# One fused transformer block with mixture of experts: token weights folded in pieces, beta in four column groups, and a reordered opening

## The chip, the cores and the metric

The kernel runs on one core of one Trainium2 chip. The metric is the device time of one execution in microseconds. The kernel before takes 736.07 us (median of 3 runs, 735.96 to 736.86). The engines are TensorE (PE, with its weight loads PEld), VectorE (DVE), ScalarE (ACT), GpSimd (POOL) and SyncE (SP), which issues all loads and stores.

## What is computed

The input is 32 images of 128x128x3. The reference does three steps, all in float32:

```
tokens = patchify(concat(x, x shifted by one pixel in 4 directions), 16)    # 64 tokens x 3840 features per image
h = layernorm(tokens, eps 1e-3) * gamma + beta;  h = h @ W + b              # 192 wide
h = h + attention(layernorm(h))     # 12 heads of 16, each 64x64, three softmax kernels (here equal),
                                    # inverse of the middle one by 6 Newton steps
h = h + experts(layernorm(h))       # 16 experts of width 128 (8) and 256 (8), top 8, gelu
```

## The kernel before

Tokens go in 16 tiles of 128 (two images each). The five shifts are not made in memory: the weights W of the five taps are scaled by gamma and summed into one small weight `weff` of 8 chunks of 128 rows, of which 6 are inner pixels and 2 are borders (the "halo"). One more column of `weff` gives the mean. `wsh[:, hh, f, ch]` is half `hh` of the pixels, tap `f`, colour `ch`; chunk `3 * hh + ch` is folded from the five taps f, by VectorE, with the semaphore `folded` counting the 32 operations. The term beta @ W is a chain of 32 matmuls with one column of weights each into row 0 of PSUM bank A; VectorE copies the row to `crow`, TensorE spreads it over 128 partitions, and VectorE adds the bias to give `cvec`. `wsum`, the column sums of `weff`, comes from 8 matmuls with a matrix of ones. An fp32 matmul is two records in the trace.

Each engine has its own program, written out by hand, and they meet by semaphores. After this prologue each runs `iteration(t)`, in which six Newton steps k of tile t are interleaved with work of its neighbours: in the windows of the steps stand the token matmul of tile t + 3 (`tok`, L263), its sums and squares, the hidden value and its normalisation for tile t + 2 (`hidden`, `normed`, then `transpose_xl`, `qk`, `value`, `masked_keys`), the scores, softmax and start matrix of tile t + 1 (`scores`, `less_max`, `transpose_kernel`, `column_sums`, `gram`, `start_newton`), and output and router of tile t - 1. The iterations begin at t = -3, with no Newton work before t = 0. Banks A to D are shared: the scores write all four, so `tok` of a later tile waits for `less_max` (semaphore `sdiff`). The rsqrt steps run on GpSimd, six small operations each.

SyncE issues all loads in one order: gamma and beta (`gbs`, 32 KB), the two halves of the taps (1440 KB each), the halo weights (192 KB), the bias spread over the partitions (96 KB), constants (169 KB), transposed x and x of tile 0 (512 KB each), the table of copies (512 KB), seven attention weights (880 KB together), the pair for tile 1, the expert weights (5376 KB), and then the pairs of tiles 2 to 15, each behind a wait for the token matmul and the squares of the tile two before. After the last tile come the experts, 24 chunks for each of four groups of tiles.

Of the kernel before, what the change touches and what calls it, by code (L numbers as in the profile page):

```python
# [11 lines left out]
CH = 8  # L12
# [28 lines left out]
def vit_block_kernel(nc, x, xt, ws, wh, gb, tok_b, wqk, wv, wp, bp, rw, w1, w2, const, copies, out):  # L41
    with ExitStack() as ctx:
# [18 lines left out]
        crow = sb("crow", [1, DIM])  # L61
# [64 lines left out]
        const_loaded, wsh_top_loaded, wsh_loaded, mult_loaded = sems("const_loaded wsh_top_loaded wsh_loaded mult_loaded")  # L126
# [25 lines left out]
        @block.sync  # L152
        def _(sp):
            def tile_loads(t):
                b = t % 2
                if t >= 2:
                    sp.wait_ge(tok_done, t - 1)
                sp.dma_start(xtb[:, b], xt[t]).then_inc(xt_loaded[b], 16)
                if t >= 2:
                    sp.wait_ge(sq_ready, t - 1)  # L160
                sp.dma_start(xin[b], x[t]).then_inc(x_loaded[b], 16)

            sp.dma_start(gbs[:], gb).then_inc(wsh_top_loaded, 16)
            sp.dma_start(wsh[:, 0], ws[:, 0]).then_inc(wsh_top_loaded, 16)
            sp.dma_start(wsh[:, 1], ws[:, 1]).then_inc(wsh_loaded, 16)
            sp.dma_start(whalo[:], wh).then_inc(wsh_loaded, 16)
            sp.dma_start(tokb[:], tok_b.partition_broadcast(P)).then_inc(wsh_loaded, 16)
            sp.dma_start(cst[:], const).then_inc(const_loaded, 16)
            tile_loads(0)
            sp.dma_start(mult[:], copies).then_inc(mult_loaded, 16)  # L170
            sp.dma_start(wqk_a[:], wqk[0:DA, :]).then_inc(attw_loaded, 16)
            sp.dma_start(wqk_b[:], wqk[DA:DA + P, :]).then_inc(attw_loaded, 16)
            sp.dma_start(wv_a[:], wv[0:DA, :]).then_inc(attw_loaded, 16)
            sp.dma_start(wv_b[:], wv[DA:DA + P, :]).then_inc(attw_loaded, 16)
            sp.dma_start(wp_sb[:], wp).then_inc(attw_loaded, 16)
            sp.dma_start(bp_sb[:], bp.partition_broadcast(P)).then_inc(attw_loaded, 16)
            sp.dma_start(rw_sb[:], rw).then_inc(attw_loaded, 16)
            tile_loads(1)
            sp.dma_start(w1_a[:], w1[0:DA, :]).then_inc(ffw_loaded, 16)
            sp.dma_start(w1_b[0:DB, :], w1[DA:DIM, :]).then_inc(ffw_loaded, 16)  # L180
            sp.dma_start(w1_b[DB:P, :], w1[DA:DIM, :]).then_inc(ffw_loaded, 16)
            sp.dma_start(w2_sb[:], w2.rearrange("(c p) n -> p c n", p=P)).then_inc(ffw_loaded, 16)
            for t in range(2, NT):
                tile_loads(t)
            with sp.Fori(0, NT // GT) as g:
                sp.wait_ge(expert_added, (g + 1) * EXPERTS + 2)
                sp.dma_start(out[bass.ds(g * GT, GT)].rearrange("t p n -> p t n"),
                             acc[:, bass.ds(g * GT, GT), :]).then_inc(out_stored, 16)
            sp.wait_ge(out_stored, 16 * (NT // GT))
# [64 lines left out]
        def _(pe):  # L254
# [142 lines left out]
            def first_window(k, t):  # L397
                if k == 0 and on(t + 1):
                    scores(t + 1)
                if k == 1 and on(t - 1):  # L400
                    out_heads(t - 1)
                if k == 1 and on(t + 3):
                    tok(t + 3, 0, 2)
                if k == 2 and on(t + 1):
                    transpose_kernel(t + 1)
                if k == 2 and on(t + 3):
                    tok(t + 3, 2, 4)
                if k == 3 and on(t + 1):
                    transpose_sums(t + 1)
                    gram(t + 1)  # L410
                if k == 4 and on(t + 1):
                    spread_denominators(t + 1)
                if k == 5 and on(t + 2):
                    qk(t + 2)

            def second_window(k, t):
                if k == 1 and on(t - 1):
                    project(t - 1)
                if k == 2 and on(t + 3):
                    tok(t + 3, 4, CH)  # L420
# [6 lines left out]
                if k == 5 and on(t + 2):  # L427
                    value(t + 2)

            def iteration(t):  # L430
                for k in range(STEPS):
                    if on(t):
                        newton(k, 0, t, 0)
                        newton(k, 0, t, 1)
                    first_window(k, t)
# [5 lines left out]
            n = 0  # L441
            for hh in range(2):
                if hh == 0:
                    pe.wait_ge(wsh_top_loaded, 32)
                else:
                    pe.wait_ge(wsh_loaded, 48)
                for f in range(15):
                    pe.matmul(A[0:1, 0:DIM], gbs[:, 1, hh * 15 + f:hh * 15 + f + 1], wsh[:, hh, f // 3, f % 3, :],  # L448
                              start=(n == 0), stop=False)
                    n += 1  # L450
            pe.matmul(A[0:1, 0:DIM], gbs[:, 1, 30:31], whalo[:, 0, :], start=False, stop=False)
            pe.matmul(A[0:1, 0:DIM], gbs[:, 1, 31:32], whalo[:, 1, :], start=False, stop=True).then_inc(beta_done, 1)
            pe.wait_ge(crow_ready, 1)
            pe.wait_ge(ones_set, 1)
            pe.matmul(B[:, 0:DIM], ones[0:1, :], crow[:], start=True, stop=True).then_inc(cbc_done, 1)
            pe.wait_ge(folded, 32)
            pe.wait_ge(mean_set, 1)
            for c in range(CH):
                last = pe.matmul(D[:, 0:DIM], ones[:], weff[:, c, 0:DIM], start=(c == 0), stop=(c == CH - 1))
            last.then_inc(wsum_done, 1)  # L460
# [4 lines left out]
            for t in range(-3, NT + 1):  # L465
# [42 lines left out]
        def _(act):  # L508
# [72 lines left out]
            def first_window(k, t):  # L581
# [6 lines left out]
                if k == 5 and on(t + 2):  # L588
                    copy_q(t + 2)

            def second_window(k, t):
# [10 lines left out]
                if k == 5 and on(t + 2):  # L602
                    copy_value(t + 2)

            def iteration(t):
                for k in range(STEPS):
                    if on(t):
                        newton(k, 0, t, 0)
                        newton(k, 0, t, 1)
                    first_window(k, t)  # L610
# [5 lines left out]
            act.wait_ge(zeros_set, 2)  # L616
            for t in range(-3, NT):
# [21 lines left out]
        def _(dve):  # L639
# [141 lines left out]
            def window(k, t):  # L781
# [4 lines left out]
                if k == 1 and on(t - 1):  # L786
                    residual_norm(t - 1)
                if k == 2 and on(t + 1):
                    dve.wait_ge(kt_done, 2 * t + 4)
                    column_sums(t + 1, B, 4, 2, colsum_b)  # L790
                if k == 2 and on(t + 2):
# [18 lines left out]
                if k == 5 and on(t + 2):  # L810
# [4 lines left out]
            def iteration(t):  # L815
                for k in range(STEPS):
                    if on(t):
                        newton_sum(k, t, 0)
                        newton_sum(k, t, 1)
                    if on(t) and k == STEPS - 1:  # L820
# [6 lines left out]

            n = 0
            for hh in range(2):
                if hh == 0:  # L830
                    dve.wait_ge(wsh_top_loaded, 32)
                else:
                    dve.wait_ge(wsh_loaded, 48)
                for f in range(5):
                    for ch in range(3):
# [9 lines left out]
                        n += 1  # L845
            for c in range(2):
# [131 lines left out]
```

## Time and profile before

| | |
|---|---|
| median of 3 runs | 736.07 us |
| the profiled execution's own time | 739.34 us |
| its span, first to last instruction | 737.6 us |
| TensorE matmul busy | 680.3 us |
| VectorE busy | 496.5 us |
| ScalarE busy | 356.3 us |
| GpSimd busy | 108.2 us |
| mean granted TensorE clock | 0.981 |

Times of the rows are microseconds from the start of the span, and those marked mean are nanoseconds. An engine's share is an average over the span; which engine sets the time in a stretch is read from the chain of waits, which follows the last instruction back to what released it at each step.

### The profile page before, as it was taken

To read this page: it belongs to the slowest core of one execution; us is meant where nothing else is said; L and a number is where in the kernel's file an instruction comes from. 1 tells how busy PE (TensorE), PEld (TensorE's weight loads), DVE (VectorE), ACT (ScalarE), POOL (GpSimd) and SP (SyncE) were. 2 spreads that over 40 slices of the span, in tenths; PEclk is the share of its full clock that TensorE was granted. 3 is DMA by queue.
4 is the path that set the end of the run, shared out by engine and by line. 5 is a ranking of instruction groups with operands and counts; after the bars stand their busy time and mean duration, and the time that the engine had idled before them with its cause. 6 is when DMAs were issued, how large, how long until landed. Compare 5 with 4: busy or idle time off the path is not lost.

```text
span 737.6 us, 30455 instructions
## 1 busy us (share of the span) xinstructions
PE 680.3 (92%) x13218; PEld 595.5 (81%) x13218; DVE 496.5 (67%) x1354; ACT 356.3 (48%) x921; POOL 108.2 (15%) x328
## 2 busy tenths in 40 slices
PE   5668999999999999999999999869999999999996
PEld 2457888788888888888888878748898898998986
DVE  5257778777878878877778877447456546646644
ACT  0125664655655655555555655534334344434432
POOL 0122123123123123223123211110000000000000
PEclk9969999999999999999999999979999999999999
DMA  8951111011011011111000000000000000000000
GB/s 311 300 182 60 61 48 44 33 44 48 33 60 33 32 60 32 32 61 32 32 4 5 4 4 4 4 1 2 1 1 21 0 0 21 0 0 21 0 0 22
DMA packets 12244, 30.48 MB, mean 41 GB/s; under 512 B 1120, under 2 KB 7392, under 8 KB 11616
## 3 DMA queue, kind: packets, MB, share of 16 engines
q1 hardware_dynamic: 12128, 28.73, 11.9%
q8 instruction: 97, 1.59, 0.9%
q14 instruction: 19, 0.16, 0.1%
HBM read 27.16 MB, written 1.57 MB: 39 GB/s over the span
## 4 chain that ended last, share of the span: by engine, by line
PE 76%; DVE 14%; ACT 5%; issue 3%; DMA 1%; POOL 1%; DVEq 0%; ACTq 0%; SPq 0%; POOLq 0%
PE ps L364 24%; PE ps L493 17%; PE ps L484 15%; PE ps L263 6%; DVE uu L734 3%; DVE sq L653 2%; PE ps L277 2%; PE ps L382 2%; PE ps L314 2%; DVE rf L741 2%; ACT qq L557 2%; PE ps L448 2%; PE ps L278 1%; ACT rr L561 1%; PE ps L375 1%
## 5 line engine op out<-in xcount | busy, mean ns | idle before, releaser
L884 DVE SCALAR_TENSOR_TENSOR acc<-ps,comb,acc 128x192 f32 x256 | 89.2, 411 | 90.3 <-PE ps L493 90.3
L493 PE MATMUL ps<-w_sb,work 128*128 128x192 f32 x768 | 139.9, 326 | 0.5 <-ACT work L633 0.3
L364 PE MATMUL ps<-rr 64*64 64x64 f32 x3840 | 131.4, 221 | 6.0 <-issue 3.3
L493 PEld LDWEIGHTS ps<-w_sb,work 128*128 128x128 f32 x768 | 129.2, 189 | 9.5 <-issue 1.7
L364 PEld LDWEIGHTS ps<-rr 64*64 64x64 f32 x3840 | 119.8, 136 | 18.7 <-ACT rr L561 10.6
L557 ACT ACTIVATE qq<-ps 128x384 f32<-128x384 f32 x192 | 92.3, 490 | 66.7 <-PE ps L364 64.7
L734 DVE SCALAR_TENSOR_TENSOR uu<-rr,qq 128x384 f32<-128x384 f32 x160 | 87.9, 559 | 50.8 <-ACT qq L557 44.6
L633 ACT ACTIVATE work<-ps 128x512 f32<-128x512 f32 x96 | 57.3, 597 | 133.6 <-PE ps L484 133.6
L561 ACT ACTIVATE rr<-ps 128x384 f32<-128x384 f32 x160 | 73.9, 490 | 80.6 <-PE ps L364 79.8
L364 PE MATMUL ps<-uu,qq 64*64 64x64 f32 x4608 | 96.6, 224 | 16.1 <-DVE uu L734 13.9
L364 PEld LDWEIGHTS ps<-uu,qq 64*64 64x64 f32 x4608 | 80.6, 134 | 33.9 <-DVE uu L734 30.6
L263 PE MATMUL ps<-weff,xtb 128*128 128x193 f32 x256 | 53.9, 347 | 3.9 <-DVE se L690 2.4
L484 PE MATMUL ps<-xhi,wah 128*128 x96 | 47.5, 495 | 1.1 <-ACT rt L579 1.1
L263 PEld LDWEIGHTS ps<-weff,xtb 128*128 128x128 f32 x256 | 42.7, 197 | 6.8 <-issue 4.7
L484 PE MATMUL ps<-xhi,wal 128*128 x96 | 38.2, 398 | 0.0
L484 PE MATMUL ps<-xhi,wb 128*128 x96 | 38.1, 397 | 0.0
L484 PE MATMUL ps<-xlo,wah 128*128 x96 | 38.1, 397 | 0.0
L484 PE MATMUL ps<-xlo,wb 128*128 x96 | 37.9, 394 | 0.0
L863 DVE TENSOR_TENSOR wal<-w_a,wah 128x128 fp32r<-128x128 f32 x98 | 28.1, 286 | 8.6 <-ACT wb L622 6.5
L863 DVE TENSOR_TENSOR wb<-w_b,wb 64x128 fp32r<-64x128 f32 x98 | 28.4, 290 | 3.1
L206 POOL TENSOR_SCALAR st<-st 128x1 f32<-128x1 f32 x16 | 6.4, 402 | 162.5 <-DVE st L653 162.5
L622 ACT ACTIVATE wah<-w_a 128x128 fp32r<-128x128 f32 x98 | 29.6, 302 | 0.0
(136 smaller groups left out, 1026.8 us busy)
## 6 DMA issues: line engine op xcount, KB each, us to landing
xtb<-xt_dram SPq DMA_DIRECT2D x16, 512.0 KB, 3.5
work<-x_dram SPq DMA_DIRECT2D x16, 512.0 KB, 3.4
wsh<-ws_dram SPq DMA_DIRECT2D x2, 1440.0 KB, 7.8
w_sb<-w_dram SPq DMA_DIRECT2D x1, 2304.0 KB, 26.3
w_a<-w_dram SPq DMA_DIRECT2D x1, 1536.0 KB, 13.2
w_b<-w_dram SPq DMA_DIRECT2D x2, 768.0 KB, 17.7
out_dram<-acc SPq DMA_DIRECT2D x4, 384.0 KB, 2.7
mult<-copies_dram SPq DMA_DIRECT2D x1, 512.0 KB, 12.8
```

Of the source, the lines that this page charges most:

```text
L263: last = pe.matmul(C[:, 0:DIM + 1], xtb[:, t % 2, c, :], weff[:, c, :], start=(c == 0), stop=(c == CH - 1))
L277: pe.matmul(D[:, w * P:w * P + P], wqk_a[:, w * P:w * P + P], xlt[:, 0, :], start=True, stop=False)
L364: last = pe.matmul(ps[z:z + 64, 2 * lane + i, 64 * j:64 * j + 64], lhs[r, lane, i, j, :], rhs[r, lane, i, j, :], start=True, stop=True)
L484: last = pe.matmul(ps[:, c % 2, :], w[:, k, :], xs[:, half, tok], start=(n == 0), stop=(n == 4))
L493: last = pe.matmul(ps[:, 2 + 2 * (e % 2) + j // 2, (j % 2) * DIM:(j % 2 + 1) * DIM], hid[:, c % 4, j * P:(j + 1) * P], w2_sb[:, c, :], sta ...
L557: act.activation(qq[:, lane].rearrange("p i h n -> p i (h n)"), ps[:, 2 * lane:2 * lane + 2, 0:LC], ACT.Copy).then_inc(q_ready, 1)
L561: act.activation(rr[:, lane].rearrange("p i h n -> p i (h n)"), ps[:, 2 * lane:2 * lane + 2, 0:LC], ACT.Copy, scale=0.25).then_inc(r_ready, 1)
L622: act.activation(w[:, c % 3, :], raw[:, c % HID * P:(c % HID + 1) * P], ACT.Copy).then_inc(whi_ready, 1)
L633: act.activation(hid[:, c % 4, :], ps[:, c % 2, :], ACT.Gelu_apprx_tanh).then_inc(gelu_done, 1)
L734: dve.scalar_tensor_tensor(out=uu[:, lane], in0=src[:, lane], scalar=3.0, in1=qq[:, lane], op0=ALU.mult, op1=ALU.add).then_inc(u_ready, 1)
L863: dve.tensor_tensor(w[a:P, k, :], raw[a:P, col:col + P], high[a:P, k, :].bitcast(F32), ALU.subtract).then_inc(wlo_ready, 1)
L884: last = dve.scalar_tensor_tensor(out=a, in0=ps[:, 2 + 2 * (e % 2) + j // 2, (j % 2) * DIM:(j % 2 + 1) * DIM].unsqueeze(1), scalar=comb[:, ...
```

## The change

The taps are loaded in ten pieces of 288 KB, each with its own semaphore, and the fold and the beta matmuls wait for each piece. Beta's 32 matmuls use a weight block of 32 equal columns at one of four column positions in turn, so each column group sums eight terms over 32 partitions; `crow` becomes the whole bank, and the spread is a matmul of ones with all 128 rows, divided by 32 where the bias is added. TensorE's token matmul of tile 0 and the weight sums run in three pieces (chunks 0 to 2, 3 to 5, 6 and 7) between the halves of beta and after them, and iteration -3 falls away on TensorE and VectorE, with `token_sums(0)` and `variance(0)` written into VectorE's prologue. ScalarE does one dummy square ahead of its first iteration. Iterations before t = 0 run `tok` in one piece in window k = 1 and `hidden` ahead of the column sums. The projections, copies and masked keys of tile 1 leave iteration -1 and stand in iteration 0 behind the first squares of tile 0. The order of loads changes: constants and transposed x of tile 0 between the tap pieces, the bias later, and the pairs of tiles 2 and 3 ahead of the expert weights.

```diff
-            sp.dma_start(gbs[:], gb).then_inc(wsh_top_loaded, 16)
-            sp.dma_start(wsh[:, 0], ws[:, 0]).then_inc(wsh_top_loaded, 16)
-            sp.dma_start(wsh[:, 1], ws[:, 1]).then_inc(wsh_loaded, 16)
-            sp.dma_start(whalo[:], wh).then_inc(wsh_loaded, 16)
-            sp.dma_start(tokb[:], tok_b.partition_broadcast(P)).then_inc(wsh_loaded, 16)
+            def taps(half, f0, f1):
+                for f in range(f0, f1):
+                    sp.dma_start(wsh[:, half, f], ws[:, half, f]).then_inc(tap_loaded[half][f], 16)
+
+            sp.dma_start(gbs[:], gb).then_inc(gamma_loaded, 16)
+            taps(0, 0, 5)
+            taps(1, 0, 2)
             sp.dma_start(cst[:], const).then_inc(const_loaded, 16)
-            tile_loads(0)
+            sp.dma_start(xtb[:, 0], xt[0]).then_inc(xt_loaded[0], 16)
+            taps(1, 2, 5)
+            sp.dma_start(whalo[:], wh).then_inc(halo_loaded, 16)
+            sp.dma_start(xin[0], x[0]).then_inc(x_loaded[0], 16)
             sp.dma_start(mult[:], copies).then_inc(mult_loaded, 16)
+            sp.dma_start(tokb[:], tok_b.partition_broadcast(P)).then_inc(tokb_loaded, 16)
...
-            tile_loads(1)
+            for t in range(1, 4):
+                tile_loads(t)
...
-            for t in range(2, NT):
+            for t in range(4, NT):
                 tile_loads(t)
...
                 if k == 1 and on(t + 3):
-                    tok(t + 3, 0, 2)
+                    tok(t + 3, 0, 2 if t >= 0 else CH)
...
-                if k == 2 and on(t + 3):
+                if k == 2 and on(t + 3) and t >= 0:
                     tok(t + 3, 2, 4)
...
-                if k == 5 and on(t + 2):
+                if k == 5 and on(t + 2) and t != -1:
                     qk(t + 2)
...
                         newton(k, 0, t, 1)
+                    if t == 0 and k == 0:
+                        qk(1)
+                        value(1)
                     first_window(k, t)
...
+            def beta(n, w):
+                z = 32 * (n % 4)
+                return pe.matmul(A[z:z + 32, 0:DIM], gbs[:, 1, n:n + 1].to_broadcast([P, 32]), w, start=(n < 4), stop=(n >= 28),
+                                 tile_position=(0, z))
+
+            def beta_taps(half):
+                for f in range(5):
+                    pe.wait_ge(tap_loaded[half][f], 16)
+                    for ch in range(3):
+                        beta(half * 15 + 3 * f + ch, wsh[:, half, f, ch, :])
+
+            def first_tok(c0, c1):
+                pe.wait_ge(folded, (15, 30, 32)[c0 // 3])
+                for c in range(c0, c1):
+                    last = pe.matmul(C[:, 0:DIM + 1], xtb[:, 0, c, :], weff[:, c, :], start=(c == 0), stop=(c == CH - 1))
+                if c1 == CH:
+                    last.then_inc(tok_done, 1)
+                for c in range(c0, c1):
+                    last = pe.matmul(D[:, 0:DIM], ones[:], weff[:, c, 0:DIM], start=(c == 0), stop=(c == CH - 1))
+                if c1 == CH:
+                    last.then_inc(wsum_done, 1)
+
+            pe.wait_ge(gamma_loaded, 16)
+            beta_taps(0)
+            pe.wait_ge(ones_set, 1)
+            pe.wait_ge(mean_set, 1)
+            pe.wait_ge(xt_loaded[0], 16)
+            first_tok(0, 3)
+            beta_taps(1)
+            pe.wait_ge(halo_loaded, 16)
+            beta(30, whalo[:, 0, :])
+            beta(31, whalo[:, 1, :]).then_inc(beta_done, 1)
+            first_tok(3, 6)
+            first_tok(6, CH)
             pe.wait_ge(crow_ready, 1)
+            pe.matmul(B[:, 0:DIM], ones[:], crow[:], start=True, stop=True).then_inc(cbc_done, 1)
...
-            for t in range(-3, NT + 1):
+            for t in range(-2, NT + 1):
                 iteration(t)
...
+                    if t == 0 and k == 0:
+                        copy_q(1)
+                        copy_value(1)
...
             act.wait_ge(zeros_set, 2)
+            act.activation(st[:, 23:24], ot[:, 0, 0:1], ACT.Square)
...
+                if k == 2 and on(t + 2) and t < 0:
+                    hidden(t + 2)
...
+                    if t == 0 and k == 0:
+                        masked_keys(1)
...
             dve.wait_ge(beta_done, 1)
-            dve.tensor_copy(crow[:], A[0:1, 0:DIM]).then_inc(crow_ready, 1)
-            dve.wait_ge(cbc_done, 1)
-            dve.tensor_tensor(cvec[:], B[:, 0:DIM], tokb[:], ALU.add).then_inc(cvec_ready, 1)
+            dve.tensor_copy(crow[:], A[:, 0:DIM]).then_inc(crow_ready, 1)
             dve.wait_ge(wsum_done, 1)
             dve.tensor_copy(wsum[:], D[:, 0:DIM]).then_inc(wsum_ready, 1)
+            token_sums(0)
+            dve.wait_ge(cbc_done, 1)
+            dve.wait_ge(tokb_loaded, 16)
+            dve.scalar_tensor_tensor(out=cvec[:], in0=B[:, 0:DIM], scalar=1.0 / 32, in1=tokb[:],
+                                     op0=ALU.mult, op1=ALU.add).then_inc(cvec_ready, 1)
+            variance(0)
             dve.wait_ge(cvec_ready, 1)
-            for t in range(-3, NT):
+            for t in range(-2, NT):
                 iteration(t)
```

## Rows read from the trace of the kernel before

**Rows 1.** Chain of waits, 0 to 90 us: start, duration, what, records.

```profile
1.18 6.31 DMA wsh<-ws_dram
7.53 12.66 PE ps L448 x60
...
21.87 2.82 PE ps L459 x16
24.71 0.37 DVE wsum L854
...
28.53 1.28 ACT L512
...
31.12 1.23 DVE sq L653
...
38.48 0.47 PE ps L271
...
44.55 0.70 PE ps L306 x24
...
50.23 1.54 PE ps L314 x6
51.77 3.20 PE ps L263 x12
```

**Rows 2.** Busy times by stretch; after the engines come granted clock, DMA share, GB/s.

```profile
9.00:12.00 3.00, 3.00 (x11) 1.16 (x10) 3.00 (x11) 0.00 (x0) 0.00 (x0) 1.00 0.92 242
...
15.00:18.00 3.00, 3.00 (x20) 1.59 (x19) 3.00 (x10) 0.00 (x0) 0.00 (x0) 1.00 1.02 395
...
33.00:36.00 3.00, 0.00 (x0) 0.00 (x0) 1.38 (x5) 0.00 (x0) 1.36 (x7) 1.00 1.06 263
36.00:39.00 3.00, 0.52 (x2) 0.29 (x2) 0.78 (x2) 0.00 (x0) 1.90 (x6) 0.68 1.10 330
...
54.00:57.00 3.00, 2.46 (x63) 1.93 (x61) 1.65 (x8) 0.00 (x0) 1.52 (x6) 0.98 0.33 96
```

**Rows 3.** Timeline of SyncE's queue: start and duration of each issue.

```profile
1.65 0.42 SPq L165 DMA_DIRECT2D wsh<-ws_dram  x1
...
3.65 0.62 SPq L158 DMA_DIRECT2D xtb<-xt_dram  x1
...
9.77 0.90 SPq L177 DMA_DIRECT2D rw_sb<-rw_dram  x1
```

**Rows 4.** Loads: size and microseconds to landing, from stretches with one issue each.

```profile
gbs<-gb_dram SPq DMA_DIRECT2D x1, 32.0 KB, 1.8
...
wsh<-ws_dram SPq DMA_DIRECT2D x1, 1440.0 KB, 9.2
...
xtb<-xt_dram SPq DMA_DIRECT2D x1, 512.0 KB, 11.6
...
rw_sb<-rw_dram SPq DMA_DIRECT2D x1, 16.0 KB, 10.4
...
xtb<-xt_dram SPq DMA_DIRECT2D x1, 512.0 KB, 16.1
```

**Rows 5.** Timeline of VectorE, the fold of one half's later taps.

```profile
8.29 4.04 DVE L843 SCALAR_TENSOR_TENSOR weff<-wsh,gbs,weff 128x192 f32<-128x192 f32 x12
```

**Rows 6.** Timeline of TensorE, head outputs of tile 0 in four column groups.

```profile
90.96 0.64 PE L375 MATMUL ps<-rf,y_t 128*32 128x64 f32 x24
91.53 0.43 PE L263 MATMUL ps<-weff,xtb 128*128 128x193 f32 x1
```

**Rows 7.** Timeline, 56 to 72 us: start matrices, first squares, tile 1's maxima.

```profile
57.99 1.03 DVE L726 TENSOR_TENSOR r<-cst,m 128x384 f32<-128x384 f32 x2
...
60.28 1.61 PE L364 MATMUL ps<-r 64*64 64x64 f32 x48
...
63.14 0.69 DVE L688 TENSOR_REDUCE sst<-ps 128x8 f32<-128x512 f32 x1
```

More of the change, by code:

```diff
@@ L60, in vit_block_kernel @@
         weff = sb("weff", [P, CH, DIM + 1])
-        crow = sb("crow", [1, DIM])
+        crow = sb("crow", [P, DIM])
         ones = sb("ones", [P, P])
@@ L124, in sems @@
             return [sem(n) for n in names.split()]
-        const_loaded, wsh_top_loaded, wsh_loaded, mult_loaded = sems("const_loaded wsh_top_loaded wsh_loaded mult_loaded")
+        const_loaded, gamma_loaded, halo_loaded, tokb_loaded, mult_loaded = sems(
+            "const_loaded gamma_loaded halo_loaded tokb_loaded mult_loaded")
+        tap_loaded = [[sem(f"tap_loaded_{half}_{f}") for f in range(5)] for half in range(2)]
         x_loaded, xt_loaded = sems("x_even_loaded x_odd_loaded"), sems("xt_even_loaded xt_odd_loaded")
@@ L418, in second_window @@
                     project(t - 1)
-                if k == 2 and on(t + 3):
+                if k == 2 and on(t + 3) and t >= 0:
                     tok(t + 3, 4, CH)
@@ L426, in second_window @@
                     logits(t - 1)
-                if k == 5 and on(t + 2):
+                if k == 5 and on(t + 2) and t != -1:
                     value(t + 2)
@@ L439, in iteration @@
                     second_window(k, t)
[L441 to L451, printed above, removed]
@@ L452, in _ @@
-            pe.matmul(A[0:1, 0:DIM], gbs[:, 1, 31:32], whalo[:, 1, :], start=False, stop=True).then_inc(beta_done, 1)
-            pe.wait_ge(crow_ready, 1)
[L454 to L459, printed above, removed]
@@ L460, in _ @@
-            last.then_inc(wsum_done, 1)
+            def beta(n, w):
[7 more added lines that the diff above has]
+                        beta(half * 15 + 3 * f + ch, wsh[:, half, f, ch, :])
@@ L587, in first_window @@
                     save_y(t + 1)
-                if k == 5 and on(t + 2):
+                if k == 5 and on(t + 2) and t != -1:
                     copy_q(t + 2)
@@ L601, in second_window @@
                     squares(t + 3)
-                if k == 5 and on(t + 2):
+                if k == 5 and on(t + 2) and t != -1:
                     copy_value(t + 2)
@@ L790, in window @@
                     column_sums(t + 1, B, 4, 2, colsum_b)
-                if k == 2 and on(t + 2):
+                if k == 2 and on(t + 2) and t >= 0:
                     hidden(t + 2)
@@ L809, in window @@
                     router_max(t - 1)
-                if k == 5 and on(t + 2):
+                if k == 5 and on(t + 2) and t != -1:
                     masked_keys(t + 2)
@@ L826, in _ @@
             dve.wait_ge(scrap_set, 1)
+            dve.wait_ge(gamma_loaded, 16)
             n = 0
             for hh in range(2):
[L830 to L833, printed above, removed]
                 for f in range(5):
+                    dve.wait_ge(tap_loaded[hh][f], 16)
                     for ch in range(3):
@@ L845, in _ @@
                         n += 1
+            dve.wait_ge(halo_loaded, 16)
             for c in range(2):
```

## The prediction

> **What bounds the kernel now.** I read the page's busy shares first: TensorE is busy 680 of 738 us, as the table shows. Then the chain of waits in order of time, which shows that this share is an average over two regimes. From about 60 us on, the chain is nearly all TensorE with short VectorE links, and the change touches nothing in it but the first of sixteen tile iterations. Before that the chain is a prologue in which one engine at a time works: the first half of the token weights lands at 7.5, 60 beta matmul records run to 20.2, the weight sums run 21.9 to 24.7, tile 0's token matmul fills the time to the table load at 28.53, which takes 1.28, and so on down to tile 0's scores at 44.55 and its transposes at 50.23 [rows 1]. Third, TensorE's clock by the stretches: the records ran at 11 per 3 us at 9 to 12 us and at 20 per 3 us at 15 to 18 us, so the start is at the lower of the two levels (1.2 and 2.4 GHz) although the page grants it 1.00; the granted clock later falls within 36 to 39 (0.68) after 33 to 36 without a matmul and is 0.98 in 54 to 57 [rows 2]. Fourth, the issues and landings of the loads [rows 3, 4]. So what is taken from the prologue shifts all the rest, because TensorE has no slack later; what merely fills a gap there brings nothing.
>
> **The change part by part.** Times are of the one profiled execution (span 737.6, its own time 739.34); the median of the plain runs is 736.07, 3.27 lower. I take the difference over to the median unchanged.
>
> *Taps instead of halves.* The halves landed at 1.18 + 6.31 = 7.5 and 1.65 + 9.2 = 10.85 [rows 1, 3, 4]: 1440 KB in 3.4 us, so 288 KB in 0.67 us. Ten issues instead of two cost SyncE 0.42 each and some 0.05 between them [rows 3], less than 0.67, so the queue stays ahead. Counting back from 7.5, the first tap lands at 4.8. VectorE folds a first tap in 0.78 and a later one in 4.04 / 4 = 1.01 [rows 5], slower than they land: 4.8 + 2 x (0.78 + 4.04) + 0.55 for the halo = 15.0, where it ended at 18.7. This takes 3.7 us from the fold, but TensorE decides, next.
>
> *Beta in four column groups, tile 0's matmul and the sums between.* Tile 0's transposed x now lies behind 2217 KB instead of 3369: 7.5 + (2729 - 1472) x 0.00234 = 10.4, where it landed at 3.65 + 11.6 = 15.25 [rows 3, 4]. The first half of beta hides under the taps. At 10.4 TensorE starts chunks 0 to 2 of token matmul and sums: 12 records of 0.18 at the higher clock (2.82 / 16 for 192 columns, [rows 1]), 0.36 at the lower. I let the clock rise at 13.2 as it did before: 7.6 records by then, 4.4 after, end 13.9. Second half and halo of beta: 34 records. No row shows column groups at 192 columns; the head outputs, 128x32 weights and 64 columns, start 24 records in (0.64 - 0.22) / 23 = 0.018 each [rows 6]; three times that for three times the columns is 0.054, so 1.8 us and 15.8. Without any overlap it is 0.16 each, 5.4 us; with no cost at all it is 0. I take 1.8, the nearest row. Chunks 3 to 7: 20 records x 0.18 = 3.6, so the weight sums are ready at 19.4 instead of 24.7: -5.2 (rounded by the issue gaps). If the clock rises only near 16.6, it is 21; if the groups do not overlap, 23; if all is at the higher clock and beta is free, 16.5. The broadcast matmul grows from one row to 128 and stays 0.6 with its copy, beside the squares.
>
> On the switch between column groups and the whole array, the same rows show a group of 128x32 matmuls between 64x64 and 128x128 ones with the next token record at 91.53, 0.57 after the first of the 24, so no gap beyond a record. The Trainium skill ("TensorEngine Tiling (Array Packing)", Key Properties) says that changing the tiling mode drains TensorE. By it the three switches added here would cost three drains, by the row at most 3 x 0.22 = 0.7 us; I count none.
>
> *Token matmul off the path.* It stood from 24.71 + 0.37 to 28.3, just before the table load, behind the sums [rows 1]: -3.2. *Dummy square on ScalarE*: the 1.28 us table load goes to the start, under the loads: -1.3. With these the squares of tile 0 start at 20.1 and the variance at 21.4 instead of 31.12: -9.7. x and the copies table (landed by about 15.4) are not late. Tile 1's token matmul comes at about 21.6, when its x lands (same bytes ahead as before), ends at 24.5 and hides under tile 0's rsqrt on GpSimd.
>
> *Variance to scores*: 31.12 to 44.55 is 13.4 us, the same instructions in the same order. Of it some 5.5 us from 38.48 on are matmuls at the lower clock. They would take half as long at the higher one, -2.7; TensorE stands idle from 24.5 to 28.8 before them, as it stood (longer, 6.6 us) before, so I let the clock fall as it did. A little more of them falls behind the rise: -0.3. Scores to the normed kernel (50.18): no change.
>
> *Token matmul of tile 2 in one piece, ahead of tile 0's transposes.* It starts at about 37.3 (before, 47.6). With part at the lower clock it takes 4.4 us (2.9 to 5.8 are the ends), so the transposes start at 41.8, 1.7 after their input, where they waited for nothing. But then they run at the higher clock (0.8, not 1.54 us) and the 3.20 us of tokens behind them, which held up the sums' transpose until 54.8, are gone; what is late next is the copy and column sum, 1.2 us. From kernel ready to the first r0 tile it was 8.3 (50.2 [rows 1] to 58.5, half of the two r0 writes [rows 7]) and becomes 7.2: -1.1, between -2.5 and +0.3. The earlier hidden(1) lies beside the copies.
>
> *Tile 1's projections behind the first squares.* Before, the squares started at 60.28, 1.8 after their first input [rows 7]. Now they start at once, but 1.6 us of squares, 1.5 of q and k, 0.9 of values, the copy and the scores follow in order before tile 1's maxima: 5.2 instead of 4.6 after r0 (63.14 before): +0.6; bounds 0 and +1.0. ScalarE has the 1.1 us squares of tile 2 and the y copies queued ahead of the first quotient copy, and VectorE waits for that one.
>
> *Loads of tiles 2 and 3 ahead of the expert weights.* Tile 2's transposed x, issued once tile 0's token matmul was done (28.2), took 16.1 us behind 5.4 MB of weights and landed at 44.3 [rows 4]; now it is wanted at 37.3, so without this the gain would end there (+7). With it, it lands by 24. Tile 3's x waits on SyncE for tile 1's squares (about 31), and the expert weights behind it then land at about 53, wanted after 500. Tile 4's x lies behind them, wanted after 80. Cost 0.
>
> Sum: -9.7 - 0.3 - 1.1 + 0.6 = -10.5; of the profiled execution 739.34 - 10.5 = 728.8, of the median **725.6**.
>
> **The rivals.**
> A. *The clock stays up.* The new prologue packs TensorE's work closer, so the fall need not come before tile 0's projections (-2.7) and tile 2's tokens (-1.4). Against it stands the 4.3 us hole; for it, that 6.6 us stood there before. Gives 725.6 - 3.5, about 722.
> B. *TensorE's opening is late*: clock up at 16.6 or groups that hardly overlap, sums at 22 to 23. +3, partly given back as the clock is then up in the token matmul: about 728.5.
> C. *Small loads do not overlap: slower.* If a tap paid the whole of a small load's time (gamma and beta's 32 KB took 1.8 us from issue to landing, [rows 4]) and the next began behind it, a tap would take 1.8 + 0.67 = 2.5 us. The ten taps end near 26, and tile 0's x and the copies table, five loads further, near 38 instead of 15.4. The variance starts then, 7 us later than before, and the seven attention loads add 14 more: some 750. It decides from 2.1 us per tap, where the copies table lands at 29.8, when the squares started. Against: nine loads of 16 to 512 KB, 1904 KB in all (tile 0's x, the copies table, the seven attention loads), landed in the 4.9 us between 15.25 and 9.77 + 10.4 = 20.2 [rows 3, 4], as fast per KB as the halves. The Trainium skill ("DMA: Bandwidth & Descriptors", Bandwidth) advises batching loads to 1 MiB or more for 75% of peak, and puts 64 KB at 32% of it. By it 288 KB taps would arrive at something like half rate, and an estimate from its figures delays the queue by some 7 us, nearer B than C.
> D. *The gain isn't there*: a later wait of the prologue takes it all, such as the attention weights (20.2) or a load. All that I found are earlier than their users; 736.
>
> **How the numbers follow.** Forecast (-8.5 to -12.5) 0.70; A 0.10; B 0.12; C 0.03; D 0.03; the rest, small gains, 0.02. Less than 0.2% (1.5 us) is what a measurement can't tell from no change. Faster 0.94, same 0.03, slower 0.03. The range for 8 in 10 takes the forecast's own bounds and most of A and B: 722.3 to 729.2.
>
> **What would show it.** Fold's first record near 4.8 and its end near 15; first token record near 10.4; wsum copy at 19.5; variance at 21.4; tile 0's scores near 34.5; less_max of tile 1 near 52.5; then all as before with -10.5. Wrong if beta's records start 0.16 apart or more, if the taps land over 0.9 us apart, if tile 2's tokens wait for a load, or if the iterations from tile 1 on take longer than they did.

## The result and the profile after

| | before | changed |
|---|---|---|
| median of 6 plain runs | 736.27 us (735.48 to 738.45) | 730.61 us (728.24 to 732.48) |
| ratio, 95% interval | | 0.9918 [0.9893, 0.9944] |
| profiled execution: span | 737.6 | 726.4 |
| mean granted clock | 0.981 | 0.984 |

The change makes the kernel 5.7 us faster. I forecast 10.5 (725.6 us), with a range of 722.3 to 729.2: the sign is right, the size is not, and the range misses.

The page after, busy times:

```profile
PE 673.6 (93%) x13218; PEld 593.3 (82%) x13218; DVE 496.8 (68%) x1354; ACT 356.3 (49%) x922; POOL 109.5 (15%) x328
```

The chain of waits of the changed kernel in its first 80 us (start, duration, what, records), which answers [rows 1]:

```profile
4.97 6.65 DMA xtb<-xt_dram
...
11.87 2.27 PE ps L467 x6
14.13 1.92 PE ps L471 x6
16.06 1.92 PE ps L455 x34
17.98 1.18 PE ps L467 x6
...
20.79 0.67 PE ps L471 x4
21.48 0.36 DVE wsum L887
...
23.23 1.23 DVE sq L685
...
36.75 1.16 PE ps L315 x24
...
40.29 4.53 PE ps L272 x16
44.82 0.67 PE ps L323 x6
...
49.58 0.57 DVE r L758
50.20 2.58 PE ps L373 x48
```

The steps are there in the order in which I had put them. But the first six token records take 2.27 us and the next six on the same tile 1.18: the same work at the lower and at the higher of TensorE's two levels, 1.2 and 2.4 GHz. The scores take 1.16 where they took 0.70, and the first squares 2.58 where they took 1.61 [rows 7].

Busy times by stretch of the changed kernel, which answer [rows 2]; the third figure from the end is the granted clock:

```profile
12.00:15.00 3.00, 3.00 (x10) 3.00 (x11) 2.60 (x8) 0.00 (x0) 0.00 (x0) 1.00 1.05 411
...
27.00:30.00 3.00, 0.00 (x0) 0.00 (x0) 1.26 (x6) 0.00 (x0) 1.62 (x7) 1.00 0.58 176
30.00:33.00 3.00, 1.87 (x7) 1.47 (x8) 0.60 (x1) 1.42 (x2) 0.49 (x1) 0.51 0.00 1
...
39.00:42.00 3.00, 1.71 (x5) 1.74 (x6) 2.41 (x6) 1.05 (x2) 0.28 (x2) 0.50 1.13 287
...
48.00:51.00 3.00, 1.48 (x30) 1.18 (x31) 2.66 (x7) 1.89 (x5) 0.00 (x0) 0.92 1.09 327
51.00:54.00 3.00, 3.00 (x40) 2.88 (x37) 1.89 (x4) 1.27 (x4) 1.86 (x4) 0.51 1.11 340
```

At 12 to 15 us the page again grants 1.00 while 10 records fill 3 us, so the start is at the lower level, as before. Then the clock falls at 30, is 0.50 at 39 to 42, and falls once more near 50.5, behind TensorE's wait for r0. This last fall has no counterpart before, where tile 1's projections filled 57.9 to 60.3.

**Two traces differ by 11.2 us and the plain runs by 5.7.** The start of each tile's last Newton sum, which writes the tile `rf`, is read from VectorE's timeline. Those of tile 0 and of tile 15 split the spans:

| | to tile 0's rf | tiles 0 to 15 | rest |
|---|---|---|---|
| before | 84.56 | 396.02 | 257.0 |
| changed | 78.55 | 391.90 | 255.9 |
| difference | -6.0 | -4.1 | -1.1 |

The change touches nothing behind the first column. An even iteration is 26.56 us from rf to rf in both traces; the trace of before has five of 26.9 to 28.9. TensorE's timeline of before shows what is in them: waits for nothing that the profile names, marked issue.

```profile
131.42 1.15 PE L364 MATMUL ps<-rr 64*64 64x64 f32 x33 [0.89 <-issue]
...
159.75 0.62 PE L364 MATMUL ps<-rr 64*64 64x64 f32 x13 [0.97 <-issue]
...
```

The profiled execution of before was a long sample (739.34 against a median of 736.27) and that of the change the shortest of its six (728.24 against 730.61), so the 11.2 that seem to confirm the -10.5 of my sum do so by chance. The first column agrees with the plain runs: -6.0 here, and -4.9 with the second trace of the changed kernel (79.67, k_after below).

### The profile page after: what moved, and what is told of

It reads as the page before. It is cut to its first block, busy times and chain, and to the rows that moved or that the text cites. A ratio compares the mean times of both kernels' runs of the same rounds, so it can differ in the third digit from the quotient of the medians.

```text
span 726.4 us, 30474 instructions
## 1 busy us (share of the span) xinstructions
PE 673.6 (93%) x13218; PEld 593.3 (82%) x13218; DVE 496.8 (68%) x1354; ACT 356.3 (49%) x922; POOL 109.5 (15%) x328
## 4 chain that ended last, share of the span: by engine, by line
PE 77%; DVE 13%; ACT 4%; issue 2%; DMA 1%; POOL 1%; SPq 1%; DVEq 0%; ACTq 0%; POOLq 0%
PE ps L373 25%; PE ps L521 17%; PE ps L512 15%; PE ps L272 6%; DVE uu L766 3%; DVE sq L685 2%; PE ps L286 2%; PE ps L391 2%; PE ps L323 2%; ACT qq L585 2%; DVE rf L773 2%; PE ps L287 2%; PE ps L341 1%; ACT rr L589 1%; PE ps L384 1%
## 5 line engine op out<-in xcount | busy, mean ns | idle before, releaser
L766 DVE SCALAR_TENSOR_TENSOR uu<-rr,qq 128x384 f32<-128x384 f32 x160 | 87.8, 559 | 46.9 <-ACT qq L585 41.0
L373 PEld LDWEIGHTS ps<-uu,qq 64*64 64x64 f32 x4608 | 80.3, 134 | 32.8 <-DVE uu L766 29.5
L272 PE MATMUL ps<-weff,xtb 128*128 128x193 f32 x240 | 50.6, 347 | 3.9 <-DVE se L722 2.4
L512 PE MATMUL ps<-xhi,wah 128*128 x96 | 47.6, 495 | 1.1 <-ACT rt L607 1.1
L272 PEld LDWEIGHTS ps<-weff,xtb 128*128 128x128 f32 x240 | 39.9, 196 | 6.6 <-issue 4.5
L654 ACT ACTIVATE wb<-w_b 128x128 fp32r<-128x128 f32 x98 | 29.4, 300 | 0.0
```

Of the source, the lines that this page charges most:

```text
L272: last = pe.matmul(C[:, 0:DIM + 1], xtb[:, t % 2, c, :], weff[:, c, :], start=(c == 0), stop=(c == CH - 1))
L373: last = pe.matmul(ps[z:z + 64, 2 * lane + i, 64 * j:64 * j + 64], lhs[r, lane, i, j, :], rhs[r, lane, i, j, :], start=True, stop=True)
L512: last = pe.matmul(ps[:, c % 2, :], w[:, k, :], xs[:, half, tok], start=(n == 0), stop=(n == 4))
L654: act.activation(w[:, c % 3, :], raw[:, c % HID * P:(c % HID + 1) * P], ACT.Copy).then_inc(whi_ready, 1)
L766: dve.scalar_tensor_tensor(out=uu[:, lane], in0=src[:, lane], scalar=3.0, in1=qq[:, lane], op0=ALU.mult, op1=ALU.add).then_inc(u_ready, 1)
```

## The experiments

Milestones of the profiled executions, in us from the start (VectorE's copy of the weight sums; variance of tile 0; scores of tile 0; its kernel transposes; first squares; first maxima of tile 1):

| | sums | variance | scores | transp. | squares | max 1 | plain median | ratio [95%] |
|---|---|---|---|---|---|---|---|---|
| before | 24.7 | 31.1 | 44.6 | 50.2 | 60.3 | 63.1 | 736.27 | 1 |
| my forecast | 19.5 | 21.4 | 34.5 | 41.8 | 47.3 | 52.5 | 725.6 | |
| changed | 21.5 | 23.2 | 36.8 | 44.7 | 50.2 | 57.1 | 730.61 | 0.9918 [0.9893, 0.9944] |
| k_after | 22.3 | 24.1 | 37.5 | 45.8 | 51.3 | 58.3 | 730.66 | 0.9918 [0.9899, 0.9937] |
| e_back | 21.0 | 22.7 | 36.2 | 43.5 | 50.7 | 53.6 | 728.48 | 0.9906 [0.9871, 0.9940] |
| e_fill | 20.2 | 21.9 | 35.3 | 41.5 | 47.1 | 52.4 | 723.74 | 0.9829 [0.9809, 0.9849] |
| e_back_fill | 20.8 | 22.6 | 33.9 | 40.2 | 47.6 | 50.5 | 725.95 | 0.9859 [0.9839, 0.9878] |
| e_move_only | 23.4 | 29.9 | 42.7 | 48.9 | 57.0 | 62.4 | 737.29 | 1.0003 [0.9987, 1.0018] |
| e_halves | 21.3 | 23.0 | 36.2 | 44.8 | 50.6 | 56.0 | 730.13 | 0.9927 [0.9898, 0.9956] |
| e_onerow | 23.5 | 25.3 | 38.8 | 46.3 | 51.8 | 58.7 | 732.36 | 0.9919 [0.9891, 0.9946] |
| e_loads_late | 21.3 | 23.0 | 36.5 | 50.6 | 56.1 | 63.0 | 736.90 | 1.0009 [0.9990, 1.0028] |
| e_split | 21.9 | 23.6 | 37.1 | 43.2 | 52.1 | 57.5 | 729.97 | 0.9909 [0.9878, 0.9940] |
| e_fill_end | 22.1 | 23.9 | 36.6 | 45.3 | 50.8 | 56.3 | 726.72 | 0.9876 [0.9852, 0.9900] |
| e_best_a | 19.7 | 21.4 | 32.8 | 39.1 | 44.6 | 49.9 | 723.63 | 0.9848 [0.9816, 0.9880] |
| e_best_b | 20.1 | 21.9 | 33.2 | 39.5 | 46.9 | 49.8 | 724.50 | 0.9855 [0.9825, 0.9886] |

The runs of one kernel spread by 2 to 4 us, so ratios that differ by less than 0.3% tell nothing; the milestones do not carry that part of the spread that arises in the iterations. They have a spread of their own: k_after, the same kernel as the changed one, is 0.8 us later at the sums and 1.1 at the maxima, and e_move_only, whose code up to the sums is that of before, copies them at 23.4 and not at 24.7, as its 60 beta records take 11.54 us and not 12.66. So a step from one milestone to the next says more than where a milestone stands.

**k_after**: no edit.

> The changed kernel as it is, as the control for the others of this group and a second trace of it. Theory 1 (the clock: my prologue steps were right in order but TensorE's clock stays low or falls where I had it high) expects 5 to 7 us less than the kernel before, and the same low stretches as in the first trace: 30 to 43 us and about 50.5 to 54 us. Theory 2 (the profile of before was itself some 4 us slow in the iterations, from idle time at TensorE marked issue, and this one less) expects iterations of tiles 3 to 11 that again differ from the even 26.56 us by random amounts that don't recur in the same tiles.

730.66 us, as the first time. The clock's low stretches recur: 0.50 at 36 to 45, and 0.67 at 51 to 54. The beta groups took 2.61 us here and not 1.92, with the same twelve slow token records ahead of them (2.27 and 1.92 us), so the end of the low stretch moves between executions. That the long iterations would not recur in the same tiles was wrong: in all runs without dummy matmuls, but for the first trace of the changed kernel (27.0 and 27.2), the second one from rf to rf takes 27.6 to 27.7 and the ninth 27.4 to 27.7. What is random is the size of the others, up to 30.9 in e_fill_end, whose profiled execution took 732.65 against a median of 726.72.

**e_back**

> Changed kernel, but the projections, copies and masked keys of tile 1 back in the iteration before tile 0's Newton steps, as in the kernel before. Clock theory: these 2.4 us of matmuls fill the hole at 47.3 to 50.2 us, the clock stays up in the first squares (1.6 instead of 2.6 us) and tile 1's maxima start about 1 to 2 us sooner than 57.1: 1 to 2 us faster than the changed kernel. Rival (the move itself is a gain, since the squares start as soon as their input is there): 0.5 to 1.5 us slower than the changed kernel.

```diff
-                if k == 5 and on(t + 2) and t != -1:
+                if k == 5 and on(t + 2):
                     qk(t + 2)          # likewise value, copy_q, copy_value, masked_keys
...
-                    if t == 0 and k == 0:
-                        qk(1)
-                        value(1)       # likewise the copies and masked_keys(1)
```

2.2 us below k_after in the median, but the intervals of the ratios overlap. The trace is clearer: from the first r0 tile to tile 1's maxima it takes 53.58 - 48.44 = 5.1 us, where the changed kernel takes 57.13 - 49.58 = 7.5. TensorE's timeline of e_back:

```profile
48.38 0.49 PE L286 MATMUL ps<-xlt,wqk_a 128*128 128x128 f32 x2 [0.47 <-ACT xlt L541]
...
50.72 1.61 PE L373 MATMUL ps<-r 64*64 64x64 f32 x48
```

The squares start later (50.7, 2.3 after r0) and yet tile 1 is ready sooner: they take 1.61 us and not 2.58.

**e_fill**: 33 dummy matmuls (66 records), whose result nobody reads.

> Changed kernel with dummy matmuls (128x128 ones on 192 columns, into a free PSUM bank, read by nobody) in TensorE's waits of the prologue: one behind each tap's beta matmuls of the first half and four after them, twelve ahead of tile 0's transposes of the normed value, seven behind tile 0's scores, two behind its kernel transposes, three ahead of the first squares. Clock theory: first token pieces at 2.4 GHz (-1.5 to -2), projections of tile 0 at 2.4 GHz (-2.5), scores (-0.5), token matmul of tile 2 (-1.5, partly hidden), first squares and q, k (-1.5 to -2): 5 to 8 us faster than the changed kernel. Rival (the clock does not matter, or dummy matmuls come in the way of real ones): between 0 and 3 us slower.

```diff
+            def fill(n):
+                for _ in range(n):
+                    pe.matmul(ps[:, 0, 0:DIM], ones[:], wsh[:, 0, 0, 0, :], start=True, stop=True)
...
+                    if half == 0:
+                        fill(1)        # behind each tap in beta_taps
...
+            fill(4)                    # behind beta_taps(0)
...
+                if k == 4 and t == -2:
+                    fill(12)           # ahead of transpose_xl(0)
...
+                    if t == -1:
+                        fill(7)        # behind scores(0); fill(2) behind transpose_kernel(0), fill(3) behind transpose_xl(1)
```

6.9 us below k_after in the same group, and the intervals are apart: 0.9829 [0.9809, 0.9849] against 0.9918 [0.9899, 0.9937]. Work was added to TensorE, and what it brought shows in the matmuls behind it, which run in as little as half the time. TensorE's timeline of e_fill:

```profile
12.79 1.15 PE L481 MATMUL ps<-weff,xtb 128*128 128x193 f32 x6
13.77 1.14 PE L485 MATMUL ps<-weff,ones 128*128 128x192 f32 x6
...
23.22 4.42 PE L272 MATMUL ps<-weff,xtb 128*128 128x193 f32 x16 [2.78 <-DMA xtb<-xt_dram]
27.48 4.06 PE L463 MATMUL ps<-wsh,ones 128*128 128x192 f32 x24
...
47.05 1.61 PE L373 MATMUL ps<-r 64*64 64x64 f32 x48 [0.17 <-DVE r L773]
```

The first token pieces and the squares run at the higher level, and so do tile 0's projections (0.22 us for two records, 0.43 in the changed kernel). Tile 1's token matmul does so only in part: it waited 2.78 us for its x, the clock fell at about 23, and the twelve dummies behind it then held up tile 0's transposes by 2 us. Even so tile 1's maxima start at 52.4, where my forecast had them (52.5).

**e_back_fill**: both edits.

> The two edits together. Clock theory: with the clock held up by the dummies the place of tile 1's projections matters little; by my own count from the trace of before (+0.6 for the move) it is 0 to 1 us faster than with the dummies alone. If the move is a gain by itself, 0.5 to 1.5 us slower than with the dummies alone.

By the trace 1.9 us earlier than e_fill at tile 1's maxima, most of it from the clock at tile 1's tokens (2.86 us, not 4.42); by the plain runs 2.2 us later, 0.9859 against 0.9829, intervals that overlap. Neither 0 to 1 faster nor clearly slower: undecided here, and e_best_a and e_best_b take it up.

**e_move_only**: the kernel before with the move of tile 1's projections (the edit of e_back the other way).

> The kernel before with one part of the change alone: tile 1's projections, copies and masked keys behind tile 0's first squares. Clock theory: TensorE then stands from 57.5 to about 59, the clock falls in or behind the first squares, and tile 1's maxima start 1 to 2.5 us later than 63.1; 1 to 2.5 us slower than before. My forecast's own term for it was +0.6; if the move were a gain it would be up to 1 us faster.

1.0003 [0.9987, 1.0018]: no change. I expected 1 to 2.5 us slower. From r0 to tile 1's maxima it takes 62.35 - 56.42 = 5.9 us, where before it took 5.15, so the move costs 0.8 here, close to my term of +0.6 and within its bounds of 0 and 1.0. TensorE stands idle for 1.15 us ahead of the squares, and they take 1.61 us all the same: the clock did not fall, against what I expected.

**e_halves**

> Changed kernel with each half of the taps in one load again, the second right behind the first, and fold and beta waiting for the half. If the pieces bring their time by the early start: the fold starts at 7.5 instead of 4.5 and ends near 18 instead of 15.9, transposed x of tile 0 lands near 12.5 and the weight sums are 1 to 3 us later: 1 to 3 us slower than the changed kernel. If small loads cost rate (part of why transposed x landed at 11.6 and not at 10.4): 0 to 1 us slower only.

```diff
-                for f in range(f0, f1):
-                    sp.dma_start(wsh[:, half, f], ws[:, half, f]).then_inc(tap_loaded[half][f], 16)
+                sp.dma_start(wsh[:, half], ws[:, half]).then_inc(tap_loaded[half][0], 16)
...
-            taps(1, 0, 2)
...
-            taps(1, 2, 5)
+            taps(1, 0, 5)
```

The second half is not right behind the first, as I had written, but behind the constants and tile 0's transposed x. 0.9927 against 0.9918: the pieces bring nothing that can be measured, and the weight sums come at the same time, 21.3. TensorE's timeline of e_halves:

```profile
7.82 2.78 PE L453 MATMUL ps<-wsh,gbs 128*32 128x192 f32 x30 [7.82 <-DMA wsh<-ws_dram]
12.70 1.22 PE L465 MATMUL ps<-weff,xtb 128*128 128x193 f32 x6 [2.10 <-DVE weff L875]
13.76 1.14 PE L469 MATMUL ps<-weff,ones 128*128 128x192 f32 x6
...
17.71 1.25 PE L465 MATMUL ps<-weff,xtb 128*128 128x193 f32 x6 [1.07 <-DVE weff L875]
```

Beta's first half stands in one block of 2.8 us, and the token pieces behind it already run at the higher level, 2.1 us instead of 4.2. They start 0.8 us later, and the last fold (2 us later than in the changed kernel) holds up the next ones by 1.07. What the pieces give the fold they take from the clock.

This run also says something on the later fall. Its order is that of the changed kernel and it has no dummies, and TensorE's idle times ahead of the first squares are the same to the hundredth (1.20, 0.37 and 1.15 us). Yet the clock stays up. Busy times by stretch of e_halves:

```profile
48.00:51.00 3.00, 1.48 (x42) 1.09 (x36) 2.65 (x8) 1.51 (x3) 0.00 (x0) 1.00 1.10 327
51.00:54.00 3.00, 3.00 (x62) 2.81 (x60) 2.24 (x5) 1.74 (x7) 1.58 (x3) 1.00 1.10 337
```

The squares take 1.61 us, and tile 1's maxima come 5.4 us after their start, where the changed kernel took 6.9 and my forecast had 5.2.

**e_onerow**

> Changed kernel with beta summed in one row again (one column of weights, one row of 32 terms), all else as in the change. Its 34 records behind the first token pieces then cost 0.16 to 0.32 each instead of the 1.92 us together that the first trace shows: 5.4 us at the higher clock, so weight sums and tile 0's squares 3.5 to 4.5 us later: 3 to 5 us slower than the changed kernel. Rival (beta off the path): 0 to 1 us slower.

```diff
-                return pe.matmul(A[z:z + 32, 0:DIM], gbs[:, 1, n:n + 1].to_broadcast([P, 32]), w, start=(n < 4), stop=(n >= 28),
-                                 tile_position=(0, z))
+                return pe.matmul(A[0:1, 0:DIM], gbs[:, 1, n:n + 1], w, start=(n == 0), stop=(n == 31))
...
+            pe.matmul(B[:, 0:DIM], ones[0:1, :], crow[:], start=True, stop=True).then_inc(cbc_done, 1)
```

Median 1.7 above k_after, the ratio the same (0.9919): less than the 3 to 5 expected. The 34 records take 5.6 us instead of 1.92, 3.7 more, but the weight sums are only 1.2 to 2.1 later, as the first token pieces, behind a beta of its first half that now takes longer (30 records from 4.58 to 11.23), take 2.1 us instead of 4.2.

**e_loads_late**

> Changed kernel with the pairs of tiles 2 and 3 behind the expert weights again. My forecast said that transposed x of tile 2 lands at 44 and is wanted at about 40: the token matmul of tile 2 waits for it, 4 us later than its 40.3, and stands ahead of tile 0's transposes: 3 to 5 us slower than the changed kernel. Rival (the load is not what was late): 0 to 0.5 us slower.

```diff
-            for t in range(1, 4):
-                tile_loads(t)
+            tile_loads(1)
...
-            for t in range(4, NT):
+            for t in range(2, NT):
                 tile_loads(t)
```

6.2 us above k_after, 1.0009 [0.9990, 1.0028] of before: the whole gain is gone. The chain of waits of e_loads_late:

```profile
20.62 24.76 DMA xtb<-xt_dram
...
45.42 5.34 PE ps L271 x16
50.76 0.67 PE ps L322 x6
```

The load lands at 45.4. I had expected 3 to 5 us here; the +7 of the prediction was the nearer.

**e_split**

> Changed kernel with the token matmul of tiles 0 to 2 in the old pieces (2, 2 and 4 chunks) around the transposes, and the hidden value in its old place. My forecast priced the one piece at -1.1 us: 1 us slower than the changed kernel. Clock theory adds that one piece is a long busy stretch which lifts the clock for the transposes and the column sums: in pieces they run at the lower level, 1 to 2.5 us slower. Rival (tile 0's transposes should not wait behind 4.5 us of tokens): 0.5 to 1.5 us faster.

```diff
-                    tok(t + 3, 0, 2 if t >= 0 else CH)
+                    tok(t + 3, 0, 2)
...
-                if k == 2 and on(t + 3) and t >= 0:
+                if k == 2 and on(t + 3):          # twice; hidden back in its old place
```

0.9909, no difference. The transposes start at 43.2 instead of 44.7, right behind their input, and the sums' transpose at 48.3, 11.2 after the scores, where the changed kernel has 46.7, 9.9 after them; at r0 the difference is 1.6. By tile 1's maxima all of it is made up (20.4 us after the scores in both), since with the late tokens the granted clock is 1.00 at 51 to 54 us. The step is worth its 1.1 us and more up to r0, and 0 behind it.

**e_fill_end**: the last five dummies of e_fill only.

> Changed kernel with only the last five dummy matmuls: two behind tile 0's kernel transposes and three ahead of its first squares. If the fall of the clock at 50.5 comes from the idle time at 45.5 to 46.7 and 49 to 50.2, these hold it up: squares in 1.6 instead of 2.6 us and tile 1's maxima 1.5 to 2 us sooner, about 1.5 us faster than the changed kernel; the stretches before stay as they were. If the fall has another cause, 0.

726.72 us, 3.9 below k_after; 0.9876 [0.9852, 0.9900], which just meets the interval of k_after. Busy times by stretch of e_fill_end:

```profile
39.00:42.00 3.00, 1.83 (x6) 1.86 (x7) 2.41 (x6) 1.04 (x2) 0.58 (x3) 0.50 1.04 299
...
51.00:54.00 3.00, 3.00 (x62) 2.81 (x62) 2.48 (x5) 1.78 (x7) 1.41 (x2) 1.00 1.09 328
```

The earlier stretch is as low as it was, and 51 to 54 holds 62 records instead of 40, at 1.00. From squares to maxima it takes 5.45 us, not 6.93: 1.5 of the gain are explained, as expected; the rest of the 3.9 is in the range of the spread. This agrees with a fall that comes from the idle time around it, but one trace does not show it, since e_halves had no fall either. Over all traces in which tile 1's projections stand behind the squares and nothing fills the idle time, the squares took 1.9 to 2.6 us in four (changed, k_after, e_onerow, e_loads_late) and 1.61 in three (e_halves, e_split, e_move_only); in the six in which dummies or the projections fill it, no fall is seen. So the idle time makes the fall possible and not certain. What decides it stays open.

**e_best_a, e_best_b**: e_fill and e_back_fill with `fill(6)` behind the spread of beta and `fill(9)` instead of `fill(12)`.

> Changed kernel with the dummy matmuls of the first fill run, and two edits to them: six more behind the spread of beta (where TensorE stood at 20.6 to 23.2 and the clock fell) and nine instead of twelve ahead of tile 0's first transposes (where they were 2 us too many when the clock was low). Clock theory: no low stretch from the first token pieces on, tile 1's maxima at 50.5 to 51.5 (52.4 in the first fill run, 57.1 in the changed kernel): 0 to 2 us faster than the first fill run, about 722 to 723.5. If the clock is not what sets it, no gain, or slower by the added dummies.

> The same dummies with tile 1's projections back ahead of tile 0's Newton steps. From the profiled runs, where this order had tile 1's maxima at 50.5 against 52.4: 0.5 to 1.5 us faster than the same with the projections moved. From the plain runs of the first pair (725.95 against 723.74): up to 2 us slower.

Now no stretch of the opening is low: from 27 us on the granted clock of e_best_a is 1.00, up to a single fall within 460 to 480 us (before has one within 480 to 500). The chain of waits of e_best_a:

```profile
12.48 0.98 PE ps L481 x6
13.46 0.98 PE ps L485 x6
14.44 1.74 PE ps L467 x34
...
19.68 0.36 DVE wsum L903
...
21.43 1.23 DVE sq L701
...
36.36 2.86 PE ps L272 x16
39.23 0.67 PE ps L323 x6
...
44.60 1.61 PE ps L373 x48
```

The weight sums come at 19.68 (forecast 19.5), the variance at 21.43 (21.4), and from there to tile 0's scores it takes 11.4 us, where the changed kernel took 13.5. Tile 1's maxima start 2.5 us sooner than in e_fill (49.9), tile 0's rf 1.65 sooner (74.22 against 75.87). But the plain median is the same, 723.63: I expected 0 to 2 us less. In the profiled execution two iterations of 27.5 and 27.4 us, 27.1 and 26.8 in e_fill, took part of it back. e_best_b is level in the trace (49.8) and 0.9 us slower in the plain runs, within the spread. With the clock up, where tile 1's projections stand makes no difference that can be measured. The best versions, e_fill and e_best_a, are 12 to 12.7 us under the kernel before in their groups and 7 under the changed one.

## Why the prediction was wrong

The step that failed is the clock under the reordered matmuls. I took its level from the trace of before: it should rise at 13.2 as it did there, and the matmuls around the first squares should keep their durations. The runs show that it rises only behind the first twelve token records (near 16, in k_after later still) and, in both traces of the changed kernel, falls once more at the first squares. The term "tile 1's projections behind the first squares" was +0.6, at most +1.0, and measured +2.4 from r0 to tile 1's maxima (7.55 us for 5.15). A smaller miss, which has nothing to do with the clock, is a load that came 1.2 us late.

Between the forecast and the changed kernel lie 57.1 - 52.5 = 4.6 us at tile 1's maxima, and by term:

- *Start of the first token pieces*: forecast 10.4, measured 11.87. Transposed x landed at 4.97 + 6.65 = 11.6, 1.2 late. I had taken the rate of the large halves for everything ahead of it; the taps landed 0.7 us apart at first, then one 1.7 behind the last (VectorE's fold waited from 7.27 to 7.70). My sign of being wrong, over 0.9 us apart, came true for this one tap.
- *Clock of the opening*: "I let the clock rise at 13.2 as it did before." This is the first half of the step that failed. Before, a block of matmuls without a gap ran from 7.5; in the change the pieces come in bursts, with TensorE idle between them and from 9.3 to 11.87, and all twelve records ran at the lower level: 4.2 us instead of 3.5, +0.7. Rival B had this, with sums at 22 to 23 and +3; they came at 21.5. e_halves shows the reverse. In the end the sums were 2.0 late and the variance 1.8: 1.5 from the late start, 0.7 from the clock, and 0.4 back from steps a little shorter than I had them (chunks 3 to 7 3.5 for 3.6, variance 1.75 behind the copy for 1.9).
- *Beta in column groups*: 1.92 for 34 records, where 0.054 each gave 1.8. Right in this trace; in k_after and e_split the same 34 records took 2.6. The chunks 3 to 7 took 3.5 (3.6). No drain can be seen between the groups and the whole array: in the chain above the beta records start at 16.06 where the ones before end (14.13 + 1.92), and the next token records at 17.98.
- *Table load and token matmul off the path*: right, the variance is 1.75 behind the copy of the sums, where it was 6.4.
- *Variance to scores*: 13.5, not 13.1: all the projections ran at the lower level, as they did before, and my -0.3 for a part behind the rise did not come. *Scores to transposes*: 7.9, not 7.3, of which 0.5 are the scores at the lower level. I priced the clock for the projections and the tokens and forgot the scores.
- *Tile 2's tokens in one piece*: 4.53 (4.4); transposes to squares 5.5 (5.5). Right.
- *Tile 1's projections behind the first squares*: +0.6 was forecast, with bounds of 0 and +1.0. This term is the other half of the failure, and the larger. Squares to maxima take 6.9, not 5.2: +1.7 on top. I counted order and waits, at the durations of the row of before, and did not ask what the 2.4 us of matmuls had done for the clock while they stood in that place. The order was counted right: where the clock stayed up, squares to maxima take 5.3 to 5.4 (e_move_only, e_halves, e_split), so 1.5 of the 1.7 are the fall. e_back and e_fill_end give 2.4 and 1.5 back, by different means.
- *Loads of tiles 2 and 3*: 0 with them, +7 without. e_loads_late: +6.2. Right.

Sum: 1.8 + 0.4 + 0.6 + 0 + 1.7 = 4.5 of the 4.6. Some 3 us of it are TensorE's clock (0.7 + 0.3 + 0.5 + 1.5); most of the rest is the late x. With the clock held up, the same order of work reaches my milestones (e_fill) or passes them (e_best_a). Rival A, the clock up, was given 0.10, and its own two prices, 2.7 and 1.4, add up to 4.1, not to the 3.5 that its time takes; the case that came, a clock that falls where it had not fallen before, was not among the rivals, and that is why the range was too narrow on that side.

## What to carry to other kernels

When a change moves matmuls out of a stretch where TensorE else waits, or cuts one block of them into bursts that follow arriving data, price each later matmul at both levels of the clock, and let the range hold both: TensorE's idle time ahead of it takes part in which it gets, and two executions of the same order can differ. In a prologue with one engine at a time, dummy matmuls in TensorE's waits can be worth more than the reordering: here 7 us against 5.7. They were tried on the changed kernel only; what they bring in the old order no run shows. And do not read a gain off two profiled executions before the stretches that the change doesn't touch are shown to be equal.

## What the runs showed of the hardware

- The granted clock is given as 1.00 from the start, but the records of the first 10 us and more run at the lower level (six token records in 2.27 us, then 1.18), so a page's clock is to be checked by the records there. The Trainium skill ("TensorE: Matmul & The Clock Gate", HAM oscillation) describes idle gaps that throw a kernel back to the lower clock; the traces agree, with falls behind holes of 2.8 us (e_fill at 23) and of 4.6 and 6.6 us (changed kernel and before, ahead of tile 0's transposes). The fall at the first squares came without any such hole, behind idle times of 1.2, 0.4 and 1.15 us, and in e_halves the same idle times brought none.
- Column groups of 128x32 with 192 columns: 0.056 us per record in the changed kernel (34 in 1.92 us), 0.051 in e_best_a (34 in 1.74), against 0.165 for one column of weights at a time (e_onerow, 34 in 5.6).
- TensorE waits of 0.5 to 1.1 us marked issue in the iterations, mostly in the same two of them, and now and then a fall of the clock behind one, make a large part of the 2 to 4 us by which the runs of one kernel spread (before and e_move_only: 2.9 of the 3.2 us between their traces lie in the iterations). With 33 to 36 dummy matmuls in the program (e_fill, e_back_fill, e_best_a, e_best_b) they stand in other iterations, the sixth and seventh. What TensorE waits for there was not tried.
